# A decoder layer on one Trainium2 core: the beginning of the program rearranged, from the first loads to the first two units

## The reference

```python
def _L0_attn_ref(x, attn_qkvw, attn_qkvb, attn_ow, attn_ob):
    qkv = x @ attn_qkvw + attn_qkvb
    qkv = qkv.reshape(B, S, 3, HEADS, hd)            # 32 heads of 32
    ...
    scores = jnp.einsum('bhqd,bhkd->bhqk', q, k) * scale
    probs = jax.nn.softmax(scores, axis=-1)
    ctx = jnp.einsum('bhqk,bhkd->bhqd', probs, v)
    return ctx @ attn_ow + attn_ob
...
x = _layernorm(x + _L0_attn_ref(x, ...))
x = _layernorm(x + matmul(fake_quant(x), fake_quant(ctx_4096)))   # 8-bit rounding of both
x = _layernorm(x + _L0_ffn_ref(x, ...))              # dense layer plus top-2 of 8 low-rank experts
```

## Time and profile before

| | |
|---|---|
| median of 3 timed runs | 723.29 us (723.2 to 723.49) |
| the profiled execution, its own time | 723.71 us |
| its span | 721.9 us |
| busy: TensorE, VectorE, ScalarE, GpSimd | 98%, 65%, 59%, 39% of the span |

### The profile page before, as it was taken

One profiled execution on the slowest core, in us unless ns is written; L12 is line 12 of the kernel. 1 busy time (PEld: TensorE's weight loads), 2 busy tenths in 40 slices (PEclk: granted clock), 3 DMA queues, 4 the chain that ended last, 5 costly groups with the idle time before them and its releaser, 6 DMA issues.

```text
span 721.9 us, 11825 instructions
## 1 busy us (share of the span) xinstructions
PE 705.7 (98%) x3511; PEld 530.1 (73%) x3511; DVE 467.1 (65%) x833; ACT 426.1 (59%) x919; POOL 279.4 (39%) x206
## 2 busy tenths in 40 slices
PE   6989999999999999999999999999999999899996
PEld 5868668667677686686776866766767777788885
DVE  5887556466575574575665745567688589765574
ACT  5458668677686686776866856864567672311111
POOL 5573160170162153143134158836645643211120
PEclk9999999999999999999999999999999999999998
DMA  8666436426436335344443376836833421331101
GB/s 287 169 199 218 115 83 198 125 72 201 112 90 198 88 107 182 103 117 132 150 111 97 101 228 176 251 128 200 276 100 139 160 75 60 120 110 62 59 30 59
DMA packets 55732, 98.97 MB, mean 137 GB/s; under 512 B 10896, under 2 KB 21520, under 8 KB 54800
## 3 DMA queue, kind: packets, MB, share of 16 engines
q1 hardware_dynamic: 55408, 98.13, 44.4%
q10 hardware_dynamic: 288, 0.39, 0.2%
HBM read 56.41 MB, written 16.65 MB: 101 GB/s over the span
## 4 chain that ended last, share of the span: by engine, by line
PE 86%; issue 5%; DVE 3%; POOL 2%; SPq 2%; DMA 1%; ACT 1%; POOLq 0%; DVEq 0%; ACTq 0%
PE bank L469 55%; PE bank L595 8%; PE bank L609 8%; PE bank L565 8%; PE bank L720 3%; SPq L254 2%; PE bank L746 1%; PE bank L521 1%; DMA w_raw<-in_wqkv 1%; PE bank L735 1%; DVE st L1480 1%; POOL wb_lo L1212 1%; PE bank L705 0%; POOL xb L1220 0%; POOL mv L1201 0%
## 5 line engine op out<-in xcount | busy, mean ns | idle before, releaser
L878 ACT ACTIVATE probs<-bank 128x512 f32<-128x512 f32 x256 | 152.1, 597 | 119.6 <-PE bank L595 116.1
L1406 DVE TENSOR_REDUCE m_col<-bank 128x1 f32<-128x512 f32 x256 | 173.0, 687 | 76.7 <-PE bank L565 75.9
L883 ACT ACTIVATE bank<-bank,m_col 128x512 f32<-128x512 f32 x256 | 169.3, 661 | 17.8 <-DVE m_col L1406 16.2
L469 PE MATMUL bank<-big_hi,w_hi 128*128 128x512 f32 x384 | 157.0, 409 | 5.5 <-DVE big_lo L1301 5.5
L469 PE MATMUL bank<-big_lo,w_hi 128*128 128x512 f32 x384 | 153.0, 398 | 0.0
L469 PE MATMUL bank<-big_hi,w_lo 128*128 128x512 f32 x384 | 151.5, 394 | 0.0
L565 PE MATMUL bank<-kp,qp 96*128 96x512 f32 x256 | 101.5, 396 | 0.7 <-ACT bank L883 0.7
L595 PE MATMUL bank<-qp,kp 98*128 98x512 f32 x256 | 101.0, 398 | 0.0
L469 PEld LDWEIGHTS bank<-big_hi,w_hi 128*128 128x128 f32 x384 | 73.5, 191 | 24.3 <-DVE big_lo L1301 5.7
L469 PEld LDWEIGHTS bank<-big_hi,w_lo 128*128 128x128 f32 x384 | 73.1, 190 | 17.1
L469 PEld LDWEIGHTS bank<-big_lo,w_hi 128*128 128x128 f32 x384 | 73.7, 192 | 14.8
(11 more groups left out here) (141 smaller groups left out, 1111.4 us busy)
## 6 DMA issues: line engine op xcount, KB each, us to landing
w_raw<-in_wqkv SPq DMA_DIRECT2D x7, 1536.0 KB, 7.3
c_raw<-in_ctx SPq DMA_DIRECT2D x16, 512.0 KB, 4.0
qp<-q_hi SPq DMA_DIRECT2D x128, 64.0 KB, 2.0
kp<-k_hi SPq DMA_DIRECT2D x124, 64.0 KB, 2.0
big_raw<-in_xT SPq DMA_DIRECT2D x16, 256.0 KB, 5.9
qp<-q_lo SPq DMA_DIRECT2D x64, 64.0 KB, 2.0
c_scratch<-c_q SPq DMA_DIRECT2D x16, 256.0 KB, 2.2
r_all<-r_scratch SPq DMA_DIRECT2D x64, 64.0 KB, 2.0
```

What stands on the lines that cost most here:

```text
L469: mm = nc.tensor.matmul(dst, lhs[a], rhs[b], start=(k == 0 and n == 0) if first is None else False, stop=(k == last_k and n == 2))
L878: nc.scalar.activation(probs[:, j, t, :], bank(ST0 + i % 2), ACT.Exp).then_inc(sem["exp_ok"], 1)
L883: nc.scalar.activation(bank(max_bank(s, n)), bank(max_bank(s, n)), ACT.Exp, bias=m_col[:, n:n + 1], accum_out=l_col[:, 1 - par, n:n + 1]). ...
L1406: nc.vector.reduce_max(m_col[:, n:n + 1], bank(max_bank(s, n)), AX, negate=True).then_inc(sem["rowmax"], 1)
```

## The change

Loads: the weights lie in HBM and in `w_raw` with the k tile outside and q, k, v inside, so the q and k weights of a tile are one run of 1 KB (two of 512 B before), and those of v are pieces of 512 B. The v weights come in two transfers. The four scale transfers become one, behind k tile 5.

Unit 0 on TensorE: 36 products of 128 x 128 on a constant tile at the start; then for each k tile `first_products`, in which each of the six products waits for its own operands, high x high of q and of k first, k's accumulation ending before q's. The v products wait for each half of their weights.

Others in unit 0: ScalarE rounds the q weights too, and writes k_hi. Its queue copies only the k parts of head 0, and rounds x of the second batch entry around that. SyncE copies the k parts of head 1, and `load_w` moves up from behind head 3 to ahead of head 2. VectorE makes `quant_constants` ahead of q_hi and quantises context tile 0 at the end of step 0. GpSimd zeroes `c_sum` in two pieces between the first k splits.

Unit 1 on VectorE: `low` is cut in two, the high part after maxima 5 and 11, the low part after 6 and 12. The clip of context tile 1 moves to after maximum 13.

```diff
-            wq_v = wqkv.rearrange("g p a k c -> g p (a k c)")
+            wq_v = wqkv.rearrange("g p k a c -> g p (k a c)")
             for k in range(KT):
-                sp.dma_start(w_raw[:, 0:2, k], wqkv[0, :, 0:2, k]).then_inc(big_in[0][k], 16)
+                sp.dma_start(w_raw[:, k, 0:2], wqkv[0, :, k, 0:2]).then_inc(big_in[0][k], 16)
                 load_x(0, k)
...
+                if k == SCALES:
+                    sp.dma_start(sc[:, 0:4], scales.rearrange("n a -> a n").to_broadcast([P, 4])).then_inc(sem["const_in"], 16)
-            sp.dma_start(w_raw[:, 2], wqkv[0, :, 2]).then_inc(wv_in, 16)
+            for ks in WV_HALVES:
+                sp.dma_start(w_raw[:, ks, 2], wqkv[0, :, ks, 2]).then_inc(wv_in, 16)
...
                     wait_alone(sp, sem["lo_ok"], 2 * s + 2)
+                    if begin:
+                        pack(s, par, 1, "k")
+                        load_w()
...
                     pack(s, par, 3, "k")
-                    if begin:
-                        load_w()
...
+                def first_products(k):
+                    q_dst, k_dst = bank(PROJ1), bank(PROJ0)
+                    pe.wait_ge(sem["x_hi_ok"], k + 1)
+                    pe.wait_ge(sem["wq_hi"], k + 1)
+                    nc.tensor.matmul(q_dst, w_hi[:, 0, k, :], big_hi[:, 0, k], start=(k == 0), stop=False)
+                    pe.wait_ge(sem["w_hi_ok"], k + 1)
+                    nc.tensor.matmul(k_dst, w_hi[:, 1, k, :], big_hi[:, 0, k], start=(k == 0), stop=False)
+                    pe.wait_ge(sem["x_lo_ok"], k + 1)
+                    nc.tensor.matmul(k_dst, w_hi[:, 1, k, :], big_lo[:, 0, k], start=False, stop=False)
+                    pe.wait_ge(sem["w_split"], k + 1)
+                    mm = nc.tensor.matmul(k_dst, w_lo[:, 1, k, :], big_hi[:, 0, k], start=False, stop=(k == KT - 1))
...
+                    nc.tensor.matmul(q_dst, w_hi[:, 0, k, :], big_lo[:, 0, k], start=False, stop=False)
+                    pe.wait_ge(sem["wq_lo"], k + 1)
+                    mm = nc.tensor.matmul(q_dst, w_lo[:, 0, k, :], big_hi[:, 0, k], start=False, stop=(k == KT - 1))
...
                 if first:
                     for k in range(KT):
-                        project(k)
-                        project(KT + k)
+                        first_products(k)
...
+            pe.wait_ge(sem["idb_ok"], 2)
+            for _ in range(WARM):
+                nc.tensor.matmul(bank(CTX, 0, P), ones16[:, :], ones16[:, :], start=True, stop=True)
             steps_of(pe, step)
...
                     nc.scalar.activation(big_hi[:, b, k], big_raw[:, b, k], ACT.Identity).then_inc(sem["x_hi_ok"], 1)
+                    if b == 0:
+                        nc.scalar.activation(w_hi[:, 0, k], w_raw[:, k, 0], ACT.Copy, scale=SM_SCALE).then_inc(sem["wq_hi"], 1)
...
+                if not prev:
+                    act.wait_ge(sem["proj_done"], 1)
+                    nc.scalar.activation(k_hi[:, :], bank(PROJ0), ACT.Identity, bias=bias[:, 0, 1:2]).then_inc(sem["hi_ok"], 1)
+                    act.wait_ge(sem["hi_ok"], 2)
+                    pack_first_keys(((0, k_hi), (PACK_HI2, k_hi)))
+                    split_x(1, range(2))
+                    act.wait_ge(sem["lo_ok"], 2)
+                    pack_first_keys(((PACK_LO, k_lo),))
+                    split_x(1, range(2, KT))
...
-                    if proj and n in (5, 11):
-                        low(0 if n == 5 else 1)
+                    if begin and n == 5:
+                        dve.wait_ge(sem["proj_done"], 2)
+                        low(0, ("hi",))
+                        dve.wait_ge(sem["hi_ok"], 2)
+                        low(0, ("lo",))
+                    if begin and n == 11:
+                        low(1, ("lo",))
+                    if second and n in (5, 11):
+                        low(n // 6, ("hi",))
+                    if second and n in (6, 12):
+                        low(n // 6 - 1, ("lo",))
...
                     if begin and n == 11:
                         split_x(1, range(KT))
-                    if second and n == 2:
                         clip_context(0)
-                    if second and n == 3:
                         round_context(0)
+                    if second and n == 13:
+                        clip_context(s)
...
                 if second:
-                    clip_context(s)
                     round_context(s)
```

More of the change, by code:

```diff
@@ L127, in decoder_layer @@
         MAX = (2, 3, 7)
+        WV_HALVES = (slice(0, KT // 2), slice(KT // 2, KT))
+        WARM = 36
+        SCALES = 5
         LAST_ACT = 384
@@ L528, in project @@
                     if first:
[L529 to L534, removed]
+                        if k == 0:
+                            pe.wait_ge(sem["wv_half"], 1)
+                        elif k == KT // 2:
                             pe.wait_ge(sem["w_split"], FIRST + 2)
@@ L884, in exp_sum, with pack_first_keys @@
                                          accum_out=l_col[:, 1 - par, n:n + 1]).then_inc(sem["sum_ok"], 1)
+                def pack_first_keys(parts):
+                    for row, src in parts:
+                        act.dma_start(kp[row:row + HD, 0, 0, :].bitcast(f32), src[0:HD, :].bitcast(f32)).then_inc(packed[0], 16)
+                if not prev:
[7 more added lines that the diff above has]
+                    split_x(1, range(2, KT))
                 done, turned, third = 0, 0, isinstance(s, int) and s == 2
@@ L893, in step @@
                         done += 1
-                    if isinstance(s, int) and s == 0 and q in (16, 33):
-                        split_x(1, range(5) if q == 16 else range(5, KT))
-                def pack_first_keys(j):
-                    rows = slice(j * HD, (j + 1) * HD)
-                    for row, src in ((0, k_hi), (PACK_HI2, k_hi), (PACK_LO, k_lo)):
-                        act.dma_start(kp[row:row + HD, 0, j, :].bitcast(f32), src[rows, :].bitcast(f32)).then_inc(packed[j], 16)
-                if not prev:
-                    act.wait_ge(sem["lo_ok"], 2)
-                    pack_first_keys(0)
-                    pack_first_keys(1)
                 if proj:
@@ L1355, in step, with low @@
                 begin = isinstance(s, int) and s == 0
-                def low(piece):
+                def low(piece, parts=("hi", "lo")):
                     hi, lo = ((q_hi, q_lo), (k_hi, k_lo))[piece]
-                    wait_alone(dve, sem["proj_done"], 3 * s + piece + 1)
-                    if not isinstance(s, int) or s >= 1:
-                        for h in range(HPG):
-                            wait_alone(dve, packed[h], PACK_INC * s)
-                    nc.vector.tensor_scalar(hi[:, :], bank(PROJ1 if piece == 0 else PROJ0),
-                                            bias[:, bass.ds(g, 1), piece:piece + 1].rearrange("p a b -> p (a b)"), None, ALU.add).then_inc(sem["hi_ok"], 1)
-                    wait_alone(dve, sem["hi_ok"], 2 * s + piece + 1)
-                    nc.vector.scalar_tensor_tensor(lo[:, :], bank(PROJ1 if piece == 0 else PROJ0),
-                                                   bias[:, bass.ds(g, 1), piece:piece + 1].rearrange("p a b -> p (a b)"),
-                                                   hi[:, :].bitcast(f32), ALU.add, ALU.subtract).then_inc(sem["lo_ok"], 1)
+                    source = bank(PROJ1 if piece == 0 else PROJ0)
+                    column = bias[:, bass.ds(g, 1), piece:piece + 1].rearrange("p a b -> p (a b)")
+                    if "hi" in parts:
+                        wait_alone(dve, sem["proj_done"], 3 * s + piece + 1)
+                        if not isinstance(s, int) or s >= 1:
+                            for h in range(HPG):
+                                wait_alone(dve, packed[h], PACK_INC * s)
+                        nc.vector.tensor_scalar(hi[:, :], source, column, None, ALU.add).then_inc(sem["hi_ok"], 1)
+                    if "lo" in parts:
+                        wait_alone(dve, sem["hi_ok"], 2 * s + piece + 1)
+                        nc.vector.scalar_tensor_tensor(lo[:, :], source, column, hi[:, :].bitcast(f32), ALU.add, ALU.subtract).then_inc(sem["lo_ok"], 1)
                 def clip_context(s):
```

56 lines of the change are left out of this document (30 added, 26 removed).

## The result

The changed kernel took 726.23 us (median of 6 runs, 725.65 to 728.17), the kernel before 723.25 in the same series (722.77 to 723.49): a ratio of 1.0045, 95% interval 1.0032 to 1.0057. It is slower, by about twice what a measurement of this kernel can tell, and lies outside the forecast range. The profiled execution of the changed kernel took 725.65 (span 723.8), the fastest of the six; against the 723.71 (span 721.9) of before it is 1.94 us longer, and this is the difference that the two traces can explain line by line.

A forecast was written before the change was run, and what follows sets the result against it. TensorE, busy 98% of the span, was taken as the bound. Terms +0.2, +0.3 and -1.3 sum to -0.8 us: 723.71 profiled becomes 722.9, and the median, 0.42 lower, 722.5; range 720.4 to 724.6.

The forecast's parts named there:

- rival A: Likeliest case: unit 0's early gain is spent waiting on its copies; 721.4 to 723.8 us, chance 0.45.
- the term +0.2 for score 10: Unit 1: score 10 starts at 39.2 us where before it could start at 39.0, costing 0.2 us.
- rival C: The clock falls at the new TensorE wait before score 9: +1.7, giving 724.2 us, chance 0.11.
- q_hi of unit 0 at 17.3: Start of unit 0: VectorE starts q_hi at 17.3 us instead of 19.00, a gain of 1.7.
- the 17.2: Unit 0: the q and k products end at 16.6 to 17.2 us, against 19.4 before.
- The early v products, slack of 2.3 us: Unit 0's v products start at 17.7 us instead of 19.4; a 2.3 us wait before score 9 absorbs delays.
- Three copies and the load, +2.5 us, one issue of 1.78 kept: SyncE in unit 0: extra issues add 2.5 us, the slow issue recurs, the last copy starts at 33.6.
- It lands 2.1 later, at 35.7: Unit 0's last copy lands 2.1 us after its start, at 35.7 instead of 34.92, releasing q_hi of unit 1.
- Rival D: The moved load blocks SyncE, so later copies land 2.0 us later: +1.2, giving 724.5 us, chance 0.12.
- TensorE waits 2.3 at score 9: Unit 1: TensorE asks for score 9 at 35.6 us and waits 2.3, spending unit 0's gain.
- Rival B, the fall of the earlier trace goes, -1.7: The gain stays, for instance because an earlier clock fall costing about 1.7 us goes: 720.8 us, chance 0.26.
- The end of unit 1, +0.3 and -1.3: End of unit 1: the early clip costs 0.3 us; the 1.3 us wait for the reciprocals goes.

The follow-up runs named there:

- e6: The changed kernel with head 1's three k copies of unit 0 back on ScalarE's queue: 724.61 us, ratio 1.0016.
- e10: The changed kernel with unit 0's head 1 k copies on ScalarE, behind its fifth rounded tile, and e9's copy order: 723.81 us, ratio 1.0008.
- e14: e10 without e9's order of unit 1's copies: 724.19 us, ratio 1.0011.
- e9: The changed kernel with unit 1's k copies of heads 0 and 1 issued ahead of head 3's q copies: 727.78 us, ratio 1.0051.
- e5: The changed kernel with VectorE's quantization constants behind k_lo of unit 0 instead of ahead of q_hi: 726.86 us, ratio 1.0042.
- e1: The changed kernel with only the 1.5 MB weight load moved back behind the copies of head 3: 728.84 us, ratio 1.007.
- e2: The changed kernel with clip and rounding of unit 0's context back between the scores of unit 1: 726.01 us, ratio 1.0037.
- e7: The changed kernel with q_hi of unit 1 waiting for head 3's q copies, not its k copies: 726.08 us, ratio 1.0036.
- e3: The changed kernel with 24 dummy products ahead of the wait before score 9 of unit 1: 726.65 us, ratio 1.0033.
- e11: e10 with clip and rounding of unit 0's context also back between the scores of unit 1: 724.49 us, ratio 1.0015.
- e12: e10 with the weight load and the clip of unit 1's context back where they stood before the change: 723.58 us, ratio 1.000.
- e8: The changed kernel with the weight load and the clip of unit 1's context both back where they stood before: 725.5 us, ratio 1.0029.
- e13: The changed kernel with both e3's dummy products and e9's copy order: 725.66 us, ratio 1.0037.
- e4: The changed kernel without the 36 warm-up products: 726.96 us, ratio 1.0042.

## Why the prediction was wrong

The mechanism of rival A was right: the copies of unit 0 hold q_hi of unit 1, that holds TensorE at score 9, and the early gain is spent there; the 1.3 us wait at the end of unit 1 goes. e6, e10 and e14 show by experiment that the copies' chain decides: three issues fewer on SyncE, and by the ratios 2.1 (e6), 2.5 (e14) and 2.7 us (e10, which has e9's order as well) come back. What failed is the term +0.2 for score 10, which measured +1.34, and the fall of the clock, which the sum put at nothing (rival C, 0.11) and which measured +1.65. Of the 1.1 between +0.2 and +1.34, 0.5 is the last copy's start (the chain began 1.4 late and was 0.9 shorter than forecast), and the rest its landing.

- **q_hi of unit 0 at 17.3**: 18.70. The products of q and k ended some 0.8 later than the 17.2: tile 3 was at ScalarE at 10.02 for 9.70, and from there to its first product it took 0.97 for my 0.65, which had left out ScalarE's small rounding behind that of x. And I had put the constants at nothing. They now stand ahead of q_hi, and one of them on a single column took 1.25 us beside the first half of GpSimd's v_lo (1.30), where it took 0.16 before. The Trainium skill (SBUF — State Buffer, Who interferes with whom) says that a tensor_tensor on VectorE with both inputs in SBUF contends with GpSimd's reads; by this rule, the trace agrees. Without that operation q_hi would still be bound by the products; e5 puts the whole at 0.3 for this execution. It can be more. In e1 two of these operations were held, one beside each half of v_lo, and q_hi started 1.1 us later than in the change though its last product of q had started 0.4 earlier (17.35 for 17.74):

```profile
16.87 1.24 DVE L1345 TENSOR_SCALAR sc<-sc 128x2 f32<-128x2 f32 x1
18.15 1.20 DVE L1347 TENSOR_TENSOR sc<-sc 128x1 f32<-128x1 f32 x1
```

- **The early v products, slack of 2.3 us**: part of the slack appeared at score 3 as a wait of 1.03, as the clip and rounding of context tile 0 stand ahead of the first maxima. I had not priced this move; e2 shows that it cost nothing by itself.
- **Three copies and the load, +2.5 us, one issue of 1.78 kept**: from the first to the last copy 12.02 us before (20.77 to 32.79) and 13.59 now, +1.6. The slow issue didn't recur here. With a start 1.4 later than forecast, the last copy was 0.5 late.
- **It lands 2.1 later, at 35.7**: 2.84 later, q_hi at 36.92. I priced the load's place by its issue alone and left its bytes in the queue out. This term was mis-sized by 0.7, and e7 shows that an earlier issue doesn't avoid it. The kernel before had it in its trace: its twelve q copies issued behind the load of 33.50 went out at 0.6 each and landed after up to 7.2 us (tile qp, 36 to 45 us, below). Rival D had the place right and the mechanism wrong: SyncE's issues weren't blocked, the landings were late.

```profile
DMA to landing us min/median/max: 2.5/4.8/7.2
```

- **TensorE waits 2.3 at score 9**: 1.45, with the 1.03 above 2.5 in all; score 10 at 40.39 for the 39.2 forecast, +1.34 instead of +0.2.
- **Rival C**: it happened. A wait of 1.45 us, much shorter than the 2.4 that the forecast leaned on, was followed by 3.4 us at 1.2 GHz, +1.65. The rule of the Trainium skill cited there (TensorE: Matmul & The Clock Gate, HAM oscillation) would have made this sum +0.9, nearer than the one that I chose; but the waits in the earlier trace rows and here were for VectorE and ScalarE, not for transfers, and no fall followed the wait of 1.80 us for a copy in e3.
- **Rival B, the fall of the earlier trace rows goes, -1.7**: it went in the profiled executions of e2, e10, e11 and e12, behind a wait as long as before (2.8), and was worth nothing. TensorE was 1.1 us further ahead at 631 us and had lost it again at 634, in a wait for VectorE.
- **The end of unit 1, +0.3 and -1.3**: +0 and -1.46. The early clip took 0.68 and fitted, and the rounding was done in time, as forecast.
- **The copies of unit 1**: no step of the forecast looked at them. It followed the lateness to score 9 and stopped, though SyncE hands it on. e3, e5, e7, e8 and e14 each paid 1.7 to 2.2 us there in their profiled executions, all but e3 with a fall of the clock behind it. So a fall avoided at 40 is often only exchanged; and with both places cleared, in e13, unit 2 pays. Yet most of this wait is not the lateness. In e5, e7, e8 and e14 the last k copy of head 0 landed 3.4 to 4.1 us after its issue, where its neighbours took 2.0, and in e3 an issue was slow. With 2.0 for this copy, 0 to 0.4 us of each wait would be left (an estimate). In the change such a copy, issued at 50.05 and landed 3.7 us later, held nothing up. What delays one copy there is open. It is this one in e7 (tile kp, 47.79 to 48.3 us):

```profile
DMA to landing us min/median/max: 3.4/3.4/3.4
```

The trace explains 1.9 us and the medians differ by 3.0; the profiled execution of the change was its fastest. Two things differ from execution to execution with the same code. The first is q_hi of unit 0. In the six profiled executions in which one of the constants was held beside v_lo (the change, e2, e3, e7, e10, e11) it started at 18.39 to 19.00, in the eight in which two were held (e4, without warm-ups, among them) at 19.13 to 20.01. The second is the clock. Every run of the four series has its mean granted clock on record: it was 0.992 or 0.993 in four of the six runs of the change (0.992 in the profiled one, with falls at 40.5 and 624), and 0.995 or more in 82 of 83 runs of the kernel before. So the extra fall is not a matter of the profiled execution alone. It is not everything: the other two runs of the change had 0.995 and took 726.19 and 728.17. How the rest of the 3.0 divides is not shown.

No version beat the kernel before by more than a measurement can tell. e12 is level with it although its transposed reciprocals are 1.2 us ahead; so where does that go? At the last unit's transposition it is still 1.35 ahead (475.66 for 477.01), 0.7 at 508 us and 0.3 at 634 us, and between these places TensorE has these waits (e12, timeline):

```profile
476.32 0.73 PE L616 MATMUL bank<-qp,kp 98*128 98x512 f32 x2 [0.39 <-DMA qp<-m_row]
...
621.46 0.50 PE L473 MATMUL bank<-bt_hi,hwT_hi 128*128 128x512 f32 x1 [2.80 <-DVE hwT_lo L1624]
632.82 0.33 PE L807 MATMUL bank<-ident,hw 128*128 128x128 f32 x1 [0.97 <-DVE hw L1614]
```

The second is 2.80 for 2.44 before. The third is new, and takes back no more than what the missing fall had given. There the clock did not fall at 622 as in the earlier trace rows, TensorE was 1.4 ahead at 631, and then waited for VectorE. What makes VectorE late there was not tried.

## What to carry to other kernels

A head start is worth only what the next chain of small transfers leaves of it: follow the lateness of a serial queue through every consumer, into the next two rounds of the loop, before pricing the first wait. A large load moved ahead of small copies on one queue cost their landing here, not their issue; look at both in the trace of before. And a new TensorE wait of 1.5 us or more is to be priced with a fair chance of 1.7 us on top, for a fall of the clock.

## What the runs showed of the hardware that I had not expected

- In the sixteen traces a fall of the granted clock to 0.50 came with waits of TensorE of 1.45, 1.71, 1.78, 2.00, 2.20, 2.28, 2.32 and 3.71 us, each for 3.4 us, and with one of 2.26 (e9) for 6.8 us; at 622 us it came with twelve of sixteen waits of 2.4 to 2.8. No fall followed the 1.80 of e3 or any wait of 1.30 or less up to 700 us.
- 64 KB copies issued behind a 1.5 MB load on the same queue landed after 2.7 to 6.8 us in the change, without a load ahead after 2.0 (e8).
- A VectorE operation on one column with two inputs in SBUF took 1.25 us instead of 0.16 beside a GpSimd subtraction of 1.30 us, and GpSimd's scaling of c_raw 2.50 at 25.53, with VectorE's subtractions running, for 1.20 at 39.27 in the same trace.
- Single issues on SyncE take 1.3 to 2.0 us instead of 0.6 now and then, at other places in each execution (27.79 before, 43.58 in e3; one of the two of 48.41, together 2.05, in e7), and single copies land after 3.4 to 4.1 us instead of 2.0.
